# Rsqrt refinements of two norms moved from VectorE to GpSimd, with the spreads behind them moved by half a step

## The reference

```python
x = x + conv_block(ln_c(x), ...)        # ln_c: (v - mean) / sqrt(var + 1e-6) over the 64 channels of a pixel
                                        # conv_block: u + w2 @ relu(w1 @ groupnorm(u)), the ffts cancel
t = to_tokens(x)                        # (8, 16384, 64)
n = (t - mean(t)) / sqrt(var(t) + 1e-5) # ln_t, per token
logits = n @ gate_w.T + gate_b          # (8, 16384, 32)
vals, idx = top_k(softmax(logits, over tokens), 8)
pooled = sum_k vals * n[idx];  h = gelu([pooled, 1] @ weight1[e]);  out = [h, 1] @ weight2[e]
t[idx] += vals * out
```

## Time and profile before

| what | value |
|---|---|
| median of 3 runs | 597.01 us (593.67 to 597.5) |
| the profiled execution | 596.93 us, of which its span is 594.8 us |
| busy in the span | PE 471.5 us (79%), DVE 468.2 us (79%), ACT 421.4 us (71%), POOL 272.9 us (46%) |
| chain that ended last | PE 33%, DVE 31%, issue 13%, ACT 12%, POOL 8% |

### The profile page before, as it was taken

The page is one execution under the profiler, slowest core; times in us unless marked ns, Lnnn a source line. Parts: engine busy times, 40 slices in busy tenths (PEclk is TensorE's granted clock), DMA queues, the critical chain, the costliest instruction groups (busy, mean ns, idle before and its releaser), DMA issues.

```text
span 594.8 us, 12859 instructions
## 1 busy us (share of the span) xinstructions
PE 471.5 (79%) x4964; PEld 191.1 (32%) x4964; DVE 468.2 (79%) x830; ACT 421.4 (71%) x645; POOL 272.9 (46%) x340
## 2 busy tenths in 40 slices
PE   6767799989988997889789888887887776756810
PEld 1322333333333332333233233332332222346510
DVE  7845775898699879988997898789979997796300
ACT  3765799899879977999799978985875475650200
POOL 1027370344009324833471456145777682014774
PEclk9659999999889989999999998898988896775955
DMA  7995477867656865786477746651127821010000
GB/s 283 349 422 190 140 248 255 280 212 218 214 207 213 238 214 188 219 257 250 158 237 229 280 146 212 213 213 72 72 83 203 233 79 71 1 42 6 14 13 8
DMA packets 36475, 106.85 MB, mean 180 GB/s; under 512 B 5176, under 2 KB 6200, under 8 KB 32320
## 3 DMA queue, kind: packets, MB, share of 16 engines
q1 hardware_dynamic: 34368, 105.00, 52.2%
q0 software_dynamic: 2048, 1.05, 1.0%
HBM read 71.95 MB, written 34.08 MB: 178 GB/s over the span
## 4 chain that ended last, share of the span: by engine, by line
PE 33%; DVE 31%; issue 13%; ACT 12%; POOL 8%; DMA 1%; DVEq 0%; ACTq 0%; POOLq 0%
PE st L430 8%; POOL out_rows L1730 5%; PE tl L478 5%; ACT junk L882 5%; PE cv L441 5%; DVE xs L1101 4%; PE tl L457 4%; PE cv L449 4%; DVE top_i L1192 4%; DVE lg L1089 4%; DVE cnd L1187 4%; DVE tok L1108 4%; POOL xs L1628 3%; PE bc L552 3%; DVE us L1093 2%
## 5 line engine op out<-in xcount | busy, mean ns | idle before, releaser
L1628 POOL TENSOR_TENSOR xs<-xs,us 128x1024 f32<-128x1024 f32 x64 | 151.0, 2379 | 104.7 <-DVE gsum L1093 41.3
L1101 DVE SCALAR_TENSOR_TENSOR xs<-cv,vecs,xs 128x1024 f32<-128x1024 f32 x64 | 82.0, 1281 | 19.4 <-PE cv L449 18.9
L449 PE MATMUL cv<-hid,w2bd 64*64 64x512 f32 x512 | 73.1, 643 | 19.2 <-ACT hid L828 18.8
L828 ACT ACTIVATE hid<-cv,b1n 128x1024 f32<-128x1024 f32 x64 | 70.9, 1108 | 21.1 <-PE cv L441 20.8
L441 PE MATMUL cv<-us,w1n 64*64 64x512 f32 x512 | 72.1, 635 | 10.4 <-DVE xs L1101 10.3
L1108 DVE STREAM_TRANSPOSE tok<-xs 128x1024 f32<-128x1024 f32 x64 | 79.5, 1241 | 0.7
L1093 DVE CUSTOM_DVE_ANT_0 us<-us,bc 128x1024 f32<-128x1024 f32 x60 | 72.6, 1211 | 3.9 <-PE bc L552 2.4
L478 PE MATMUL tl<-xs,gcen 128*32 128x256 f32 x1024 | 74.9, 414 | 0.8 <-ACT us L835 0.8
L882 ACT ACTIVATE junk<-us 128x1024 bf16<-128x1024 f32 x64 | 67.5, 1054 | 3.5 <-DVE gsum L1093 1.8
L858 ACT ACTIVATE sqx<-xs 128x1024 f32<-128x1024 f32 x64 | 66.4, 1049 | 2.1 <-PE st L430 1.9
L552 PE MATMUL bc<-rstd_s,spread 32*128 32x256 f32 x368 | 48.5, 342 | 21.5 <-DVE lg L1089 7.4
(11 more groups left out here) (254 smaller groups left out, 647.8 us busy)
## 6 DMA issues: line engine op xcount, KB each, us to landing
us<-in_raw SPq DMA_DIRECT2D x64, 512.0 KB, 5.1
xs<-in_x SPq DMA_DIRECT2D x32, 1024.0 KB, 4.9
out_rows<-tok SPq DMA_DIRECT2D x64, 512.0 KB, 4.8
us<-in_e_w SPq DMA_DIRECT2D x8, 260.0 KB
xs<-in_e_w SPq DMA_DIRECT2D x8, 256.0 KB
sqc<-out_rows,idx_all POOLq DMA_INDIRECT x32, 3.0
out_rows<-sqc,idx_all POOLq DMA_INDIRECT x32, 2.1
vecs<-in_b SPq DMA_DIRECT2D x4, 0.2 KB, 6.8
```

Of the source, the lines that this page charges most:

```text
L449: mm = pe.matmul(cv[C * h:C * h + C, CH * sl:CH * sl + CH], w2bd[r, r], hid[r, CH * h:CH * h + CH], start=True, stop=True)
L828: nc.scalar.activation(hid[:], cv[:], ACT.Relu, bias=b1n[:, par:par + 1]).then_inc(h_done, 1)
L1101: nc.vector.scalar_tensor_tensor(out=xu, in0=cv[:], scalar=vecs[:, 3:4], in1=xu, op0=ALU.add, op1=ALU.add).then_inc(x1_done, 1)
L1628: nc.gpsimd.tensor_tensor(xu, xu, su, ALU.add).then_inc(s_done, 1)
```

## The change

`rstd` (from image 1 on) and `ln2_rstd` (images 0 to 6) leave DVE. DVE keeps one instruction of `rstd`, `rstd_begin`, which reads the sums from PSUM and writes (v + eps) * y into SBUF (`na`, the buffer `lnv`); the variance of ln2 is now written into `lnv` too. GpSimd does the rest in SBUF: six instructions for ln1, seven for ln2, each waiting for the one before. The GpSimd merge is split into `merge_best`, which ACT waits for, and `merge_places`, which now comes after the refinements and `candidates`; a copy on DVE (the M job) waits for the places of the merge before. L0 to L2 all move into step 2, S0 and S1 to the middle and the end of step 3, and ACT squares units 0 and 1 in step 4. The tail's two ln2 refinements and image 0's ln1 stay on DVE.

```diff
-S_JOBS = {(3, 0): 0, (3, 1): 1, (4, 0): 2, (4, 1): 3, (5, 0): 4, (5, 1): 5, (6, 0): 6, (6, 1): 7}
-L_JOBS = {(1, 2): 0, (2, 0): 1, (2, 1): 2, (7, 0): 3}
+S_JOBS = {(3, 1): 0, (3, 2): 1, (4, 0): 2, (4, 1): 3, (5, 0): 4, (5, 1): 5, (6, 0): 6, (6, 1): 7}
+L_JOBS = {(2, 0): 0, (2, 1): 1, (2, 2): 2, (7, 0): 3}
-LAST_L_JOBS = {(1, 2): 0, (2, 0): 1, (2, 1): 2, (3, 1): 3}
+LAST_L_JOBS = {(2, 0): 0, (2, 1): 1, (2, 2): 2, (3, 1): 3}
...
@@ ScalarE, step
-                if s >= 1:
+                if s >= 1 and s != 4:
                     square_at(it, (s - 1, 2))
...
+                if s == 4:
+                    square_at(it, (s - 1, 2))
@@ VectorE
+                    wait(dve, idx_out, k)
...
+            def rstd_begin(n):
+                dve.wait_ge(y0_ready, n + 2)
+                nc.vector.scalar_tensor_tensor(out=na[:], in0=sums_of(n, 1), scalar=EPS_C, in1=y0[:],
+                                               op0=ALU.add, op1=ALU.mult).then_inc(na_ready, 1)
...
-                if s == 1 and t >= 0:
-                    ln2_rstd(t)
...
-                    rstd(n)
+                    rstd_begin(n)
@@ GpSimd
+            def refine(a, y, out):
+                cp(nc.gpsimd.tensor_tensor(a, a, y, ALU.mult))
+                cp(nc.gpsimd.tensor_scalar(a, a, -0.5, 1.5, ALU.mult, ALU.add))
+                cp(nc.gpsimd.tensor_tensor(a, a, y, ALU.mult))
+                cp(nc.gpsimd.tensor_copy(hi[:], a))
+                cp(nc.gpsimd.tensor_scalar(y, hi[:].bitcast(F32), second[:], None, ALU.mult))
+                return nc.gpsimd.tensor_tensor(out, y, a, ALU.add)
+            def rstd(n):
+                pool.wait_ge(na_ready, n)
+                refine(na[:], y0[:], rstd_s[:]).then_inc(rstd_ready, 1)
+            def ln2_rstd(f):
+                pool.wait_ge(y2_ready, f + 1)
+                cp(nc.gpsimd.tensor_tensor(lnv[:], lnv[:], y2[:], ALU.mult))
+                refine(lnv[:], y2[:], rstd2_s[:]).then_inc(rstd2_ready, 1)
...
                 if it >= 3:
-                    merge_places(it - 3)
+                    merge_best(it - 3)
+                ln2_rstd(it - 1)
+                if it >= 3:
                     merge_values(it - 3)
+                if it + 1 < NB:
+                    rstd(it + 1)
                 if it >= 2:
                     candidates(it - 2)
+                if it >= 3:
+                    merge_places(it - 3)
```

More of the change, by code:

```diff
@@ L174, in mk_metaformer_kernel @@
         tb = sb("tb", [P, 20])
-        y2 = y0
+        y2, na = y0, lnv
         gsum = sb("gsum", [P, NU])
@@ L264, in mk_metaformer_kernel @@
         msq_done, var2_ready, ln2_done, y2_ready = (sem(n) for n in ("msq_done", "var2_ready", "ln2_done", "y2_ready"))
+        na_ready = sem("na_ready")
         ln2_steps, rstd2_ready = sem("ln2_steps"), sem("rstd2_ready")
@@ L300, in variance2 @@
         def variance2(f):
-            return st2[:, SUB:2 * SUB] if f < NB - 1 else lnv[:]
+            return lnv[:]
         def sums_of(n, part):
@@ L484, in x1_sums @@
                 if m == 0:
-                    wait(pe, rstd2_ready, b)
+                    wait(pe, var2_ready, b)
                 if m == 2 and b == NB - 1:
@@ L502, in xc_square_sums @@
                 if m == 0:
-                    pe.wait_ge(rstd_ready, n + 1)
+                    pe.wait_ge(na_ready if n >= 2 else rstd_ready, n - 1 if n >= 2 else n + 1)
                 sum_group(st1[:, SUB:2 * SUB], sqc, m, SQC, m == 0, CH, SUB).then_inc(sumsq_done, 1)
@@ L1159, in ln2_variance @@
                 dve.wait_ge(msq_done, f + 1)
-                v2, var = variance2(f), st2[:, SUB:2 * SUB] if f < NB - 1 else variance2(f)
+                v2, var = variance2(f), variance2(f)
                 link(nc.vector.scalar_tensor_tensor(out=var, in0=st2[:, SUB:2 * SUB], scalar=EPS, in1=ta[:],
@@ L1173, in ln2_rstd @@
                                                op0=ALU.mult, op1=ALU.add).then_inc(rstd2_ready, 1)
-                assert link.n == LN2_STEPS * (f + 1), link.n
             def search_base(t):
@@ L1321, in last_step @@
                     top_places(NB - 3, 2)
-                if s == 1:
-                    ln2_rstd(t)
                 if s == 3:
@@ L1648, in halve, with merge_best @@
                     cp(nc.gpsimd.tensor_tensor(v[:, :, 0:n], v[:, :, 0:n], v[:, :, n:2 * n], ALU.add))
-            def merge_places(m):
+            def refine(a, y, out):
[12 more added lines that the diff above has]
+                refine(lnv[:], y2[:], rstd2_s[:]).then_inc(rstd2_ready, 1)
+            def merge_best(m):
                 pool.wait_ge(best_ready, m + 1)
@@ L1659, in merge_places @@
                 nc.gpsimd.tensor_tensor(gbm[:, 1:2], gate_bias[:], gbm[:, 0:1], ALU.subtract).then_inc(bias_ready, 1)
+            def merge_places(m):
                 for f in range(GATHERS):
@@ L1682, in _ @@
                 add(0, k)
+            rstd(1)
             for k in range(6):
@@ L1686, in _ @@
                 if it >= 3:
-                    merge_places(it - 3)
+                    merge_best(it - 3)
+                ln2_rstd(it - 1)
+                if it >= 3:
                     merge_values(it - 3)
+                if it + 1 < NB:
+                    rstd(it + 1)
                 if it >= 2:
                     candidates(it - 2)
+                if it >= 3:
+                    merge_places(it - 3)
                 if it == NB - 1:
                     gather(4)
+                    merge_best(it - 2)
                     merge_places(it - 2)
```

## The result

| | before | changed kernel |
|---|---|---|
| median | 595.34 us (588.91 to 597.5) | 607.11 us (604.65 to 607.22) |
| ratio | | 1.021, 95% interval 1.015 to 1.027 |
| span of the profiled execution | 594.8 us | 605.4 us |

The change makes the kernel 2.1% slower. The prediction said 605.8 us, slower. Its sum is right to about 2 us; several of its terms are not.

The account below looks back on a forecast made before the run. No engine's total work was taken to set the time; DVE held steps 1 to 4. From 597, +0.5 (round 0), +2.0 (round 1), +1.6 (rounds 2 to 5), +4.8 (rounds 6, 7) gave 605.9, written 605.8; range 591 to 614 us.

Parts of the forecast that it names:

- The sign and the sum: Whole kernel: slower, 605.8 us from 597 by adding terms per round; slower was given 0.5.
- x: Time of a one-tensor 128x256 instruction in GpSimd's refinements: taken as 0.73 us, bounds 0.33 and 1.05.
- slope of 24: Whole kernel: the one-tensor instruction's time x stands about 24 times on the path.
- dividing line of x = 0.61: Whole kernel: the one-tensor price x at which the slowdown passes 1%, deciding between slower and same.
- The first rival: GpSimd's refinements: cheap one-tensor instructions, ln2 4.4 to 4.9 us, time 596 to 602; chance with its neighbourhood 0.36.
- The template up to x1 of step 4: Middle rounds 2 to 5: chain from ln2's start value through L0 puts x1 0.4 us later, +1.6 in all.
- where 2.0 stood: Before x1 of step 4: S0 lying between adds 1.2 us, VectorE's wait for S1's spread 0.8.
- the 4 forecast: VectorE in steps 2 to 4: idle about 4 us per round, waiting out the work removed.
- The step that failed: Steps 1 to 4: VectorE holds them; lateness or gain at x1 of step 4 passes whole to the round's end.
- Rounds 6 and 7: GpSimd's queue: round 7's ln2 refinement waits behind the gathers, TensorE stands at L0, +4.8 us coming through whole.
- The second rival: All rounds: the work taken from VectorE comes through, about 577 us, half of it 590; chance 0.14.

Follow-up runs that it names:

- experiment 2: Changed kernel with the ln2 refinement of round 7 alone made by VectorE again, ahead of x1 of step 1; 602.18 us, 1.012 of the kernel before.
- experiment 4: Kernel before with the change's new S and L tables and squares, both refinements staying on VectorE; 624.42 us, 1.049 of the kernel before.
- experiment 9: Kernel before with only S0 and S1 half a step later and their squares in step 4; 612.48 us, 1.033 of the kernel before.
- experiment 1: Changed kernel with S0, S1 and their squares back at their places of before; 592.81 us, 0.998 of the kernel before.
- experiment 5: Changed kernel with S0, S1 and squares at their old places and round 7's ln2 refinement on VectorE; 590.22 us, 0.994 of the kernel before.
- experiment 6: Experiment 5's kernel with L0 to L2 of round 7 also back at their places of before; 588.45 us, 0.988 of the kernel before.
- experiment 7: Experiment 1's kernel with GpSimd's ln2 chain two instructions (1.49 us) longer in rounds 1 to 6, result unchanged; 610.07 us, 1.026 of the kernel before.
- experiment 8: Changed kernel with only ln1 on GpSimd, ln2 back on VectorE and all tables of before; 597.41 us, 1.003 of the kernel before.
- Experiment 3: Changed kernel with TensorE's logits matmuls and sums of x ahead of S3's spread in step 4; 605.05 us, 1.016 of the kernel before.

## Why the prediction was right, and where it was not

**The sign and the sum** were right: +8.9 forecast, +10.6 between the two profiled spans. But errors in opposite directions nearly cancelled, so the closeness is luck: the price of a GpSimd instruction was too high, and the clock and part of round 7 stood at nothing.

**The price of a one-tensor instruction** was too high: x is 0.58 in the mean. ln2 took 5.16 us (225.32 to 230.48) and not 5.6, L0 waited 0.65 us and not 1.1. By the prediction's own slope of 24 this alone is 3.6 us less, 602.2. That is below its dividing line of x = 0.61, on the side that it gave to "same": what made the kernel slower is not what the prediction called decisive. The first rival was right for two of the three instructions, the cast and the one with constants. The Trainium skill, page "GPSIMD Engine Reference", section "4.1 Engine selection", has one-input work at about line rate; these two (0.40 and 0.41) agree with it, the third (0.93) does not. The third's nearest row was the TENSOR_SCALAR of the earlier trace rows, which also takes a factor per row.

**The template up to x1 of step 4** held. In round 3 x1 of step 4 starts 24.23 us behind the start value of ln2 (225.25), against 24.41 before; forecast was 24.8, and 0.45 of the difference is x. The two late S jobs cost 1.85 us between x1 of step 3 and of step 4 (9.10 against 7.25), where 2.0 stood. VectorE was idle for 3.4 us between 227 and 244 (0.70, 0.50, 0.60, 0.99, 0.60), near the 4 forecast. S0 never waited for GpSimd.

**The step that failed** is that everything was measured at x1 of step 4, since "what arrives there late or early, the round's end takes over". Behind that point TensorE's clock fell: 1.5 us in step 4 of five rounds (7.55 against 6.03), 7.7 in all, which no term held. At the round's end 1.2 of each 1.5 are left (58.10 against 56.91 in round 2). Round 2, which kept its clock, takes the 56.91 us of round 4 of the kernel before, so at full clock the round breaks even, as the template said. That the loss did not show in rounds 2 to 5 of the table above comes from the kernel before, whose profiled execution has falls of its own there (step 4 of round 5 below): rounds 2 and 5 take 58.53 and 59.74 us. So rounds 2 to 5 were not alike in time.

```profile
361.32:368.89 7.57, 7.43 (x66) 2.82 (x68) 5.92 (x10) 5.92 (x10) 5.21 (x3) 0.77 0.48 134
```

How firmly fall and pause go together can be counted in step 4 of rounds 1 to 5. Where TensorE waited 2.54 or 2.55 us ahead of S3's spread (the changed kernel, experiments 2, 4 and 9) the granted clock fell in 16 of 20 steps; where it waited 0.72 or 0.73 (the kernel before, experiments 1 and 5 to 8) in 4 of 30.

**Rounds 6 and 7**: the queue on GpSimd was named rightly, and taking the refinement out of it lowers the median by 4.9 us. The term missed about 2.4. It priced TensorE's wait at L0 alone: half the clock follows the 6.38 us of it (conv2 takes 1.98 us there, 1.04 in the earlier trace rows), and ScalarE's wait for `merge_best` behind the same gathers stood at nothing. That wait holds round 7 up where ln2 has left GpSimd (experiments 5, 6 and 8). The late L jobs of round 7 may cost up to 2.9 us more (experiment 6, one profiled execution).

**The second rival** (the relief comes through) is wrong for the change and right for its parts. The prediction argued that L0 would have to be out by 226.4 to gain 2 us; experiment 1 gains 1.7 us per round at full clock with L0 as late as here. The template had S0 and S1 at their late places and so put down to GpSimd's lateness what the S table cost.

**Open**: why the clock stays in one round and falls in the next behind the same pause (2.54 us in round 2, 2.55 in round 3), and why the kernel before falls in step 4 of round 5 with the same 5.8 us of work in step 3 ahead of it as in round 4. Experiment 3 says that the fall can move; no run here shows by what rule.

## What to carry to other kernels

Price a change of place and a change of engine apart: here the engine change gained 16 to 17 us and two table edits lost 29, and one of the two was not needed. Where an engine in order waits at a shared buffer, follow the wait one step beyond the point where the lateness is measured, and look at the clock behind it. A helper engine's queue must be read in its worst round, not in a middle one, and for every engine that waits for it: the last round, with its gathers, lost 8.4 us, the four middle ones together nothing.

## What the hardware showed beyond expectation

On GpSimd a 128x256 multiplication by a column of factors takes 0.93 us, more than one of two whole tensors (0.73), while constants take 0.41. TensorE's clock fell behind a pause of 2.55 us in 16 of 20 steps, behind 0.73 us in 4 of 30, and a fall cost 1.5 us more (7.55 instead of 6.03 for a step). A mend that fills the pause moved the fall to a later step instead of removing it. Of rounds 1 to 6, four ran at a mean granted clock of 1.00 in experiments 1 and 5, two in the kernel before and one in the changed kernel.
